# A fused Griffin block and two MLPs on one core: first part reordered, root on ScalarE, first x in four transfers

## The chip, the cores and the metric

The kernel runs on one core of a Trainium2 chip. The metric is the device time of one execution in microseconds (us). A core has these engines, each working through its own instructions in order: TensorE (PE, matrix products; PEld is its weight load), VectorE (DVE), ScalarE (ACT), GpSimd (POOL) and SyncE (SP), which here only issues transfers. They wait for each other through semaphores.

## What is computed

The reference, cut to its steps, for x of 4 sequences x 1024 tokens x 256 features:

```python
t = rmsnorm(x, norm1_w)
xb = causal_depthwise_conv(t @ Wx, conv_w, conv_b)          # 4 taps
r, i = sigmoid(xb @ Wa), sigmoid(xb @ Wi)
a = exp(-8 * softplus(lam) * r)
h = scan(a, sqrt(max(1 - a*a, 1e-12)) * (i * xb))           # h[s] = a[s] h[s-1] + b[s]
h1 = x + (h * gelu(t @ Wy)) @ Wo
u = rmsnorm(h1, norm2_w)
y = h1 + (gelu(u @ Wg) * (u @ Wu)) @ Wd                     # 256 -> 1024 -> 256
x1 = layernorm(x + y)
out = layernorm(x1 + relu(x1 @ W1 + b1) @ W2 + b2)          # 256 -> 1024 -> 256
```

## The kernel before

The tokens are cut into 8 chunks of 512 (four tiles of 128 tokens, two "pairs" of tiles). The hidden width of 1024 is cut into 8 units per chunk, so that gate, up and down of the first MLP are 64 units; a period is the 8 units of one chunk. Most products are done three times in a reduced type, as high x high, high x low and low x high part of the operands: `..._hi` is the rounded tensor (written by ACT, or by POOL for `gu_hi`), `..._lo` the rest (a subtraction on DVE). Six products of 512 columns (lines L361 to L363) are one `gate` or one `up` of a unit; 12 products of 256 columns (L372 to L374) are one `down`. The weights are split into hi and lo parts too, once, while the first chunk is worked on.

There is no scheduler: each engine's order is written by hand, one block per engine. It has a **front**, in which chunk 0 goes through the mixing part (norm, conv, gates a and i, scan, y, output projection) with plain fp32 products by halves of 256 tokens, and then the rounds. `first_period(r)`, r = 0 to 7, is period 0: units 0 to 7 of chunk 0, and between them the mixing of chunk 1 and the splits of the remaining weights. `round_of(r)` is each later round.

What stands in the front, engine by engine:

- SP: chunk 0's x in two transfers of 256 KB, one per pair, then six small vectors, Wx, then x of chunk 1 (`load_x(1)`, 512 KB, issue line L301) and the other weights.
- ACT: squares with row sums of the first x (L768), copy of the vectors, `lam` terms, then the first half of the transposed t scaled (`first_tT[0]`), then `square_second_x(0)`, which waits for x of chunk 1, and behind it in the queue `first_conv_start`, which begins the conv of chunk 0. Then tanh and exp for gate a and tanh for gate i by halves, the square root for the scan's input (L1093, with a table load before it), `first_tT[1]` half, gelu of y, and splits.
- POOL: mean and reciprocal root of the squares (`first_rms`, L1587 and L1590), `lam` constants, the norm of chunk 1, `first_rms` of h1, then `add_x_h1(0)` (x + h1 for the later sum, two adds of 128x512, L1639).
- DVE: the norm of t (L1148), the other half of `first_tT[0]`, 12 conv taps (L1199), scan input and scans (L1168, L1175), the product with y (L1183), h1 (`add_mix`, L1266), weight splits (`weight_lo`, L1353 and L1355), `uT_lo` (L1142).
- PE: `first_x`, `first_gates` (L447: for each half all of a, then all of i), transposes of chunk 1's t, y (L447 too), the x product of chunk 1 (`second_x`, L414), the output projection (`first_out`, L474), more of L414, the transposes of u (L388), then unit 0.

In `first_period(r)` PE does gate(r), up(r) and, from r = 1, down(r - 1). At r = 3 it then waits until Wa and Wi are split (`split_done("a", "i")`) and does `mix_decay(1)` and `mix_input(1)`, the gates of chunk 1. On DVE round r does `gate_times_up(r)` (L1308, waits for up(r) of PE and the gelu of ACT), `gate_lo(r)` (L1313, waits for POOL's `gu_hi`), and between them parts of chunk 1's conv; at r = 2 it splits Wa, Wi and Wx behind `gate_lo(2)`.

`LAG_UP` (10) and `LAG_DOWN` (11) say by how many rounds the second MLP's products follow.

Of the kernel before, what the change touches and what calls it, by code (L numbers as in the profile page):

```python
# [10 lines left out]
P = 128  # L11
# [14 lines left out]
def griffin_mlp_kernel(nc, x, norm1_w, Wx, Wy, conv_w, conv_b, Wi, Wa, lam, Wo, norm2_w, Wg, Wu, Wd,  # L26
# [14 lines left out]
    with ctx:  # L41
# [62 lines left out]
        ln_eps = sb("ln_eps", [P, 1])  # L104
        half_c = sb("half_c", [P, KD])
# [46 lines left out]
        def x_squares(c):  # L152
            return c + 2

# [53 lines left out]
        x0_loaded = [sem(f"x0_loaded{q}") for q in range(PAIRS)]  # L208
# [7 lines left out]
        second_tT_ready = sem("second_tT_ready")  # L216
# [35 lines left out]
        u_ready = sem("u_ready")  # L252
        xh_ready = sem("xh_ready")
# [28 lines left out]
        ln_eps_ready = sem("ln_eps_ready")  # L282
        last_sd_ready = sem("last_sd_ready")
# [15 lines left out]
        def _(sync):  # L299
# [5 lines left out]
            def load_first_x(q):  # L305
                sync.dma_start(xs[0][:, 2 * q:2 * q + 2, :],
                               x_dram[0:1, :, 2 * q:2 * q + 2, :].rearrange("c p t d -> (c p) t d")
                               ).then_inc(x0_loaded[q], DMA)
# [13 lines left out]
            for q in range(PAIRS):  # L322
                load_first_x(q)
# [34 lines left out]
        def _(pe):  # L358
# [24 lines left out]
            def transposed_by_pairs(src, c, ready, done, bank, fillers):  # L383
                for q in range(PAIRS):
                    pe.wait_ge(ready, 4 * c + 2 * q + 2)
# [37 lines left out]
            def first_x():  # L423
                for h in range(2):
                    for m in range(KD):
                        pe.wait_ge(first_tT_ready[h], KD)
# [4 lines left out]
                        for k in range(KD):  # L431
                            last = nc.tensor.matmul(psum[2 * m + h][:, 0:cols.stop - cols.start],
                                                    raw_weight("x")[:, k, m * P:(m + 1) * P],
                                                    first_tT[0][:, k, cols], start=(k == 0), stop=(k == KD - 1))
                        last.then_inc(half_wx_done if h == 0 else wx_done, 1)

            def second_x(m):
                pe.wait_ge(second_tT_ready, KD)
                pe.wait_ge(tanh_i_ready, KD)
                for k in range(KD):  # L440
                    last = raw_step(psum[MIX + m][:, :], "x", m, k, first_tT[1])
                last.then_inc(wx_done, 1)
# [9 lines left out]
            def first_gates(h):  # L452
                pe.wait_ge(w_loaded["a"], DMA)
                for k in range(KD):
                    pe.wait_ge(half_taps_added if h == 0 else taps_added, taps_done(0, LOOKBACK - 1, k))
                    last = half_step(SECOND, "a", k, h, xb)
                last.then_inc(wa_done, 1)
                pe.wait_ge(w_loaded["i"], DMA)
                for k in range(KD):
                    last = half_step(MIX, "i", k, h, xb)  # L460
                last.then_inc(wi_done, 1)
# [52 lines left out]
            def transpose_u(c):  # L514
                pe.wait_ge(u_ready, 4 * c + 4)
# [10 lines left out]
            def gate_up(r):  # L526
                c, m = divmod(r, KH)
# [8 lines left out]
                product(gate_bank(r)[:, :], "g", m, uT_hi, uT_lo).then_inc(gate_done, 1)  # L536
                if r == 0:
# [123 lines left out]
            def first_period(r):  # L661

                gate_up(r)
                if r in (1, 5):

                    pe.wait_ge(hi_split["d"], 1 + r // 5)
                    pe.wait_ge(lo_split["d"], 1 + r // 5)
                if 1 <= r < KH - 1:
                    down(r - 1)
# [4 lines left out]
                if r == KH - 1:  # L674
# [6 lines left out]
                    split_done("x")  # L681
                    mix_x(2, [0])
                    transposed_by_pairs(normed, 1, u_ready, uT_done, SECOND, (0, 0))
                    mix_x(2, [1])

            def round_of(r):
                p, m = divmod(r, KH)
                n = p + 1
                mixing = n < CHUNKS
                if units(r):  # L690
# [15 lines left out]
                if r in (LAG_DOWN, LAG_DOWN + 4):  # L706
# [1059 lines left out]
```

## Time and profile before

| what | us |
|---|---|
| median of 3 runs | 599.85 |
| lowest and highest run | 599.59, 600.19 |
| the profiled execution, its own time | 600.54 |
| its span, first to last instruction | 598.7 |
| PE busy in the span | 590.6 (99%) |
| DVE, ACT, POOL busy | 381.5, 317.2, 187.1 |

Times in the rows are microseconds from the span's start. A row of the timeline is one instruction or some equal ones that follow each other: start, time from the first one's start to the last one's end, engine, line, operation, out<-in with shapes, and in brackets how long the engine was idle before it and what ended that. Matmuls overlap, so a row of PE that lasts 0.39 can be followed by the next after 0.23; a wait of PE is seen best in the distance of two starts.

### The profile page before, as it was taken

The numbers are of one execution on the slowest core, as the hardware profiler recorded it, in microseconds if no ns is written. First come the engines' busy times: TensorE is split into PE (matmuls) and PEld (weight loads), VectorE is DVE, ScalarE is ACT, GpSimd is POOL, SyncE is SP. The second block draws the span as 40 slices with busy tenths as digits, with TensorE's granted clock in tenths as the row PEclk, the third lists the DMA queues.
The fourth block names the chain that finished last, engine by engine and source line by source line (L and its number), as shares of the span: only waits on it lengthen the run. The fifth ranks groups of instructions, "written<-read, shape, count | busy, mean of one in ns | idle before, by whom it ended". The sixth has DMA issues, their size and how long they took to land.

```text
span 598.7 us, 9284 instructions
## 1 busy us (share of the span) xinstructions
PE 590.6 (99%) x3529; PEld 521.7 (87%) x3529; DVE 381.5 (64%) x700; ACT 317.2 (53%) x601; POOL 187.1 (31%) x287
## 2 busy tenths in 40 slices
PE   8999999999999999999999999999999999999996
PEld 7768888899888998889898988889888898889896
DVE  5889877374856567484774846857478474662565
ACT  5988853654438444375443744356444653323454
POOL 3041353117240352313513153140722215240130
PEclk9999999999999999999999999999999999999999
DMA  8530010001001010010100001010000100010011
GB/s 283 166 106 1 1 36 1 2 1 36 1 1 35 2 37 0 1 36 2 35 2 19 18 1 36 1 36 2 1 1 0 37 2 0 2 36 0 1 37 36
DMA packets 13100, 15.68 MB, mean 26 GB/s; under 512 B 616, under 2 KB 12288, under 8 KB 13056
## 3 DMA queue, kind: packets, MB, share of 16 engines
q1 hardware_dynamic: 13056, 15.09, 7.5%
q8 instruction: 28, 0.46, 0.3%
q14 instruction: 16, 0.13, 0.1%
HBM read 10.89 MB, written 4.19 MB: 25 GB/s over the span
## 4 chain that ended last, share of the span: by engine, by line
PE 91%; DVE 5%; ACT 1%; issue 1%; DMA 1%; POOL 1%; SPq 0%; DVEq 0%
PE psum L361 17%; PE psum L363 17%; PE psum L362 17%; PE psum L372 11%; PE psum L374 11%; PE psum L373 11%; PE psum L379 3%; DMA xs<-in_L_attn_x_dram 1%; PE psum L447 1%; PE psum L575 1%; PE psum L577 1%; PE psum L573 1%; DVE row L1285 1%; PE psum L474 1%; PE psum L414 1%
## 5 line engine op out<-in xcount | busy, mean ns | idle before, releaser
L1662 POOL TENSOR_SCALAR gu_hi<-gu_raw 128x512 fp32r<-128x512 f32 x64 | 52.8, 824 | 313.1 <-DVE gu_raw L1308 310.3
L1318 DVE TENSOR_TENSOR hid_lo<-hid_raw,hid_hi 128x512 fp32r<-128x512 f32 x56 | 45.6, 814 | 84.0 <-ACT hid_hi L952 84.0
L948 ACT ACTIVATE hid_raw<-psum,vecs 128x512 f32<-128x512 f32 x56 | 38.5, 687 | 113.8 <-PE psum L363 113.8
L1308 DVE TENSOR_TENSOR gu_raw<-psum,gu_raw 128x512 f32<-128x512 f32 x64 | 44.1, 689 | 68.4 <-PE psum L363 68.1
L372 PE MATMUL psum<-w_d_hi,gu_hi 128*128 128x256 f32 x256 | 72.8, 284 | 0.2 <-DVE gu_lo L1313 0.2
L372 PE MATMUL psum<-w_hi,hid_hi 128*128 128x256 f32 x256 | 71.7, 280 | 0.2 <-DVE hid_lo L1318 0.2
L374 PE MATMUL psum<-w_hi,hid_lo 128*128 128x256 f32 x256 | 71.8, 281 | 0.0
L374 PE MATMUL psum<-w_d_hi,gu_lo 128*128 128x256 f32 x256 | 71.8, 281 | 0.0
L373 PE MATMUL psum<-w_lo,hid_hi 128*128 128x256 f32 x256 | 71.7, 280 | 0.0
L373 PE MATMUL psum<-w_d_lo,gu_hi 128*128 128x256 f32 x256 | 71.7, 280 | 0.0
L939 ACT ACTIVATE gu_raw<-psum 128x512 f32<-128x512 f32 x64 | 38.3, 598 | 48.6 <-PE psum L363 48.0
L1313 DVE TENSOR_TENSOR gu_lo<-gu_raw,gu_hi 128x512 fp32r<-128x512 f32 x64 | 44.5, 696 | 14.7 <-POOL gu_hi L1662 14.7
L361 PE MATMUL psum<-uT_hi,w_g_hi 128*128 128x512 f32 x128 | 51.1, 399 | 0.2 <-DVE uT_lo L1142 0.2
L372 PEld LDWEIGHTS psum<-w_hi,hid_hi 128*128 128x128 f32 x256 | 48.2, 188 | 3.2 <-DVE hid_lo L1318 0.6
L372 PEld LDWEIGHTS psum<-w_d_hi,gu_hi 128*128 128x128 f32 x256 | 48.2, 188 | 3.1 <-DVE gu_lo L1313 0.7
L361 PE MATMUL psum<-uT_hi,w_u_hi 128*128 128x512 f32 x128 | 50.0, 390 | 0.3 <-DVE w_u_lo L1353 0.2
L373 PEld LDWEIGHTS psum<-w_lo,hid_hi 128*128 128x128 f32 x256 | 48.1, 188 | 2.2
L363 PE MATMUL psum<-uT_hi,w_u_lo 128*128 128x512 f32 x128 | 50.0, 390 | 0.0
L362 PE MATMUL psum<-uT_lo,w_g_hi 128*128 128x512 f32 x128 | 50.0, 390 | 0.0
L363 PE MATMUL psum<-uT_hi,w_g_lo 128*128 128x512 f32 x128 | 49.9, 390 | 0.0
L362 PE MATMUL psum<-uT_lo,w_u_hi 128*128 128x512 f32 x128 | 49.8, 389 | 0.0
L373 PEld LDWEIGHTS psum<-w_d_lo,gu_hi 128*128 128x128 f32 x256 | 48.1, 188 | 1.9
(222 smaller groups left out, 1519.3 us busy)
## 6 DMA issues: line engine op xcount, KB each, us to landing
out_dram<-row SPq DMA_DIRECT2D x15, 256.0 KB, 2.2
xs<-in_L_attn_x_dram SPq DMA_DIRECT2D x7, 512.0 KB, 3.5
raw<-in_L_ffn_W_dram SPq DMA_DIRECT2D x2, 1024.0 KB, 7.9
raw_gud<-in_L_attn_Wg_dram SPq DMA_DIRECT2D x1, 1024.0 KB, 7.4
raw_gud<-in_L_attn_Wu_dram SPq DMA_DIRECT2D x1, 1024.0 KB, 9.5
raw_gud<-in_L_attn_Wd_dram SPq DMA_DIRECT2D x1, 1024.0 KB, 12.7
xs<-in_L_attn_x_dram SPq DMA_DIRECT2D x2, 256.0 KB, 2.9
raw_xyai<-in_L_attn_Wx_dram SPq DMA_DIRECT2D x1, 256.0 KB, 2.6
```

The lines of the kernel that those rows point to most:

```text
L361: nc.tensor.matmul(dst, w_hi[n][:, k, cols], hi[:, k, :], start=(k == 0), stop=False)
L362: nc.tensor.matmul(dst, w_hi[n][:, k, cols], lo[:, k, :], start=False, stop=False)
L363: return nc.tensor.matmul(dst, w_lo[n][:, k, cols], hi[:, k, :], start=False, stop=(k == KD - 1))
L372: nc.tensor.matmul(dst, hi, w_hi[n][:, k, :], start=start, stop=False, skip_group_check=True)
L373: nc.tensor.matmul(dst, hi, w_lo[n][:, k, :], start=False, stop=False, skip_group_check=True)
L374: return nc.tensor.matmul(dst, lo, w_hi[n][:, k, :], start=False, stop=stop, skip_group_check=True)
L939: nc.scalar.activation(gu_raw[:, r % SLOTS, :], gate_bank(r)[:, :], ACT.Gelu_apprx_tanh).then_inc(gelu_ready, 1)
L948: nc.scalar.activation(hid_raw[:, w % SLOTS, :], bank[:, :], ACT.Relu, bias=vec("b1", m)).then_inc(relu_ready, 1)
L1308: nc.vector.tensor_tensor(gu_raw[:, r % SLOTS, :], up_bank(r)[:, :], gu_raw[:, r % SLOTS, :], ALU.mult).then_inc(gu_ready, 1)
L1313: nc.vector.tensor_tensor(gu_lo[:, r % SLOTS, :], gu_raw[:, r % SLOTS, :], gu_hi[:, r % SLOTS, :].bitcast(FP32), ALU.subtract).then_inc(gu ...
L1318: nc.vector.tensor_tensor(hid_lo[:, w % SLOTS, :], hid_raw[:, w % SLOTS, :], hid_hi[:, w % SLOTS, :].bitcast(FP32), ALU.subtract).then_inc ...
L1662: nc.gpsimd.tensor_scalar(gu_hi[:, r % SLOTS, :], gu_raw[:, r % SLOTS, :], 1.0, 0.0, ALU.mult, ALU.add).then_inc(gu_hi_ready, 1)
```

## The change

The front:

- The first x comes in four transfers of 128 KB, tiles 0 and 2 from SP's queue, 1 and 3 from ACT's.
- The reciprocal root of the first x's mean square is a Sqrt on ACT and a reciprocal on DVE, instead of two POOL instructions. ACT gets a table load for Sqrt first and one for Exp behind the copy of the vectors.
- DVE and ACT exchange the halves of `first_tT[0]`; the `lam` steps of DVE come behind it.
- `first_gates` does a and i of feature half k together, k = 0 then k = 1. `second_x` is cut by k: k = 0 of both m before `first_out(0)`, k = 1 of m = 0 between the two `first_out`, k = 1 of m = 1 behind them.
- On DVE `first_scan_input(1)` and `first_scan(1, 0)` come later; the last tile of u's norm is done by DVE instead of ACT, ahead of `weight_lo("u", ks=[0])`.
- `add_x_h1(0)` of POOL moves from the end of the front behind `gate_hi(3)`.

Period 0 and after:

- PE does gate(1) before up(0), and down(r - 2) between gate(r) and up(r) instead of down(r - 1) behind up(r). The transposes of u of chunk 1 go by pairs around `mix_x(2, [0])`.
- Unit 11 has the order gate, down, up, then a, W1, i, W2; at unit 10 DVE takes `gate_times_up` earlier; `uT_lo` of chunk 1 stands before both statistics.

```diff
@@ SP: first x @@
-            for q in range(PAIRS):
-                load_first_x(q)
+            for tt in (0, 2):
+                load_first_x(tt)
@@ PE: first_gates @@
                 pe.wait_ge(w_loaded["a"], DMA)
+                pe.wait_ge(w_loaded["i"], DMA)
                 for k in range(KD):
                     pe.wait_ge(half_taps_added if h == 0 else taps_added, taps_done(0, LOOKBACK - 1, k))
-                    last = half_step(SECOND, "a", k, h, xb)
-                last.then_inc(wa_done, 1)
-                pe.wait_ge(w_loaded["i"], DMA)
-                for k in range(KD):
-                    last = half_step(MIX, "i", k, h, xb)
-                last.then_inc(wi_done, 1)
+                    last_a = half_step(SECOND, "a", k, h, xb)
+                    last_i = half_step(MIX, "i", k, h, xb)
+                last_a.then_inc(wa_done, 1)
+                last_i.then_inc(wi_done, 1)
@@ PE: first_period @@
-                gate_up(r)
-                if r in (1, 5):
-
-                    pe.wait_ge(hi_split["d"], 1 + r // 5)
-                    pe.wait_ge(lo_split["d"], 1 + r // 5)
-                if 1 <= r < KH - 1:
-                    down(r - 1)
+                if r != 1:
+                    gate(r)
+                if r == 0:
+                    gate(1)
+                if r in (2, 6):
+
+                    pe.wait_ge(hi_split["d"], 1 + r // 6)
+                    pe.wait_ge(lo_split["d"], 1 + r // 6)
+                if r >= 2:
+                    down(r - 2)
+                up(r)
@@ PE: end of the front @@
-            second_x(0)
+            for m in range(KD):
+                second_x(m, 0)
             pe.wait_ge(w_loaded["o"], DMA)
             for q in range(PAIRS):
                 first_out(q)
-            second_x(1)
+                second_x(q, 1)
@@ ACT: square_first_x @@
+                    act.wait_ge(rms_eps_ready, 1)
+                    act.wait_ge(x_squared, q + 1)
+                    nc.scalar.activation(rstd1[:, tiles], ss1[:, tiles], ACT.Sqrt, bias=rms_eps[:, :],
+                                         scale=1.0 / D).then_inc(rms1_ms, 1)
@@ ACT: front @@
+            for tt in (1, 3):
+                act.dma_start(xs[0][:, tt:tt + 1, :],
...
+            act.preload_act_table(ACT.Sqrt)
             square_first_x()
...
+            act.preload_act_table(ACT.Exp)
@@ DVE: first_norm_t @@
+                nc.vector.reciprocal(rstd1[:, tiles], rstd1[:, tiles]).then_inc(rms1_rstd, 1)
@@ DVE: front, scans @@
-            for h in range(2):
-                first_scan_input(h)
+            first_gated_input(1)
+            first_scan_input(0)
             for m in range(KD):
                 first_scan(0, m)
-            first_scan(1, 0)
+            first_scan_input(1)
             first_gated(0)
-            first_scan(1, 1)
+            for m in range(KD):
+                first_scan(1, m)
@@ DVE: front, end @@
             dve.wait_ge(rms2_rstd, 2)
+            dve.wait_ge(tT_done, 4)
+            nc.vector.tensor_scalar(normed[:, TT - 1, :], h1[0][:, TT - 1, :], rstd2[:, TT - 1:TT], None,
+                                    ALU.mult).then_inc(last_u_ready, 1)
             weight_lo("u", "n2", ks=[0])
@@ POOL: round_of @@
                     gate_hi(r)
+                    if r == 3:
+                        add_x_h1(0)
@@ POOL: front @@
             first_rms(0, ss2, h1_squared, rms2_ms, rstd2, rms2_rstd)
-            add_x_h1(0)
```

What stands in a row on PE where unit 0 ends and unit 1 begins; `psum0` and `psum4` take gate(0) and gate(1), `psum1` and `psum5` up(0) and up(1). Before:

```order
L363 MATMUL psum0<-uT_hi,w_g_lo 128x512
L361 MATMUL psum1<-uT_hi,w_u_hi 128x512
L362 MATMUL psum1<-uT_lo,w_u_hi 128x512
L363 MATMUL psum1<-uT_hi,w_u_lo 128x512
L361 MATMUL psum1<-uT_hi,w_u_hi 128x512
L362 MATMUL psum1<-uT_lo,w_u_hi 128x512
L363 MATMUL psum1<-uT_hi,w_u_lo 128x512
L361 MATMUL psum4<-uT_hi,w_g_hi 128x512
```

and after:

```order
L371 MATMUL psum0<-uT_hi,w_g_lo 128x512
L369 MATMUL psum4<-uT_hi,w_g_hi 128x512
L370 MATMUL psum4<-uT_lo,w_g_hi 128x512
L371 MATMUL psum4<-uT_hi,w_g_lo 128x512
L369 MATMUL psum4<-uT_hi,w_g_hi 128x512
L370 MATMUL psum4<-uT_lo,w_g_hi 128x512
L371 MATMUL psum4<-uT_hi,w_g_lo 128x512
L369 MATMUL psum1<-uT_hi,w_u_hi 128x512
```

gate(1) has moved in front of up(0).

PE in round 3, ahead of the gates of chunk 1 (`mT_hi`, `w_a_hi`); `psum3` takes down, `psum5` up(3). Before:

```order
L374 MATMUL psum3<-w_d_hi,gu_lo 128x256
L372 MATMUL psum3<-w_d_hi,gu_hi 128x256
L373 MATMUL psum3<-w_d_lo,gu_hi 128x256
L374 MATMUL psum3<-w_d_hi,gu_lo 128x256
L361 MATMUL psum6<-mT_hi,w_a_hi 128x512
```

and after:

```order
L371 MATMUL psum5<-uT_hi,w_u_lo 128x512
L369 MATMUL psum5<-uT_hi,w_u_hi 128x512
L370 MATMUL psum5<-uT_lo,w_u_hi 128x512
L371 MATMUL psum5<-uT_hi,w_u_lo 128x512
L369 MATMUL psum6<-mT_hi,w_a_hi 128x512
```

Ahead of `mix_decay(1)` stood three downs, the last right before it; now two stand there, and down(2) comes in round 4.

POOL at the end of the front and in period 0, `h_0` being the sum of x and h1 of chunk 0. Before:

```order
L1590 TENSOR_TENSOR rstd<-rstd,minus_half 128x2
L1639 TENSOR_TENSOR h_0<-h_0,xs 128x512 x2
L1625 COPY xtail<-xv 128x6
L1662 TENSOR_SCALAR gu_hi<-gu_raw 128x512 x6
L1595 TENSOR_SCALAR rstd<-ss 128x4
```

and after:

```order
L1657 TENSOR_TENSOR rstd<-rstd,minus_half 128x2
L1692 COPY xtail<-xv 128x6
L1731 TENSOR_SCALAR gu_hi<-gu_raw 128x512 x4
L1708 TENSOR_TENSOR h_0<-h_0,xs 128x512 x2
L1731 TENSOR_SCALAR gu_hi<-gu_raw 128x512 x2
```

The two adds have moved behind four of the `gu_hi`.

## Rows read from the trace of the kernel before

**Rows 1.** The page: its head and part 1, busy time of each engine.

```profile
span 598.7 us, 9284 instructions
PE 590.6 (99%) x3529; PEld 521.7 (87%) x3529; DVE 381.5 (64%) x700; ACT 317.2 (53%) x601; POOL 187.1 (31%) x287
```

**Rows 2.** Stretches from:to: length, busy us (instructions) by engine, PE clock, DMA share, GB/s.

```profile
38.00:82.00 44.00, 43.80 (x257) 38.29 (x258) 37.58 (x60) 34.91 (x68) 13.25 (x16) 1.00 0.09 35
82.00:110.00 28.00, 27.48 (x142) 22.59 (x142) 17.69 (x31) 12.81 (x23) 11.04 (x16) 1.00 0.06 19
110.00:560.00 450.00, 449.88 (x2716) 401.35 (x2715) 275.15 (x494) 220.65 (x407) 143.28 (x212) 1.00 0.04 13
```

**Rows 3.** The chain that ended last, in the front: start, us, engine, what.

```profile
4.09 4.87 DMA xs<-in_L_attn_x_dram
...
20.44 1.28 ACT L1093
21.73 0.64 ACT xv L1093
```

**Rows 4.** Timeline of the first 14 us, all engines.

```profile
3.52 0.42 ACT L768 ACTIVATE decay<-xs 128x256 f32<-128x256 f32 x1 [1.52 <-DMA xs<-in_L_attn_x_dram]
...
7.38 0.84 ACT L1076 ACTIVATE first_tT<-psum,vecs 128x256 f32<-128x256 f32 x2 [1.11 <-PE psum L388]
...
8.99 0.42 ACT L788 ACTIVATE inp<-xs 128x256 f32<-128x256 f32 x1 [0.77 <-DMA xs<-in_L_attn_x_dram]
...
12.14 1.10 PE L447 MATMUL psum<-xb,raw_xyai 128*128 128x256 f32 x4
...
13.47 0.70 PE L447 MATMUL psum<-xb,raw_xyai 128*128 128x256 f32 x2 [0.23 <-DVE xb L1199]
```

**Rows 5.** Timeline of 14 to 40 us, DVE at the end of the front.

```profile
25.65 0.67 DVE L1183 TENSOR_TENSOR gy<-gy,xv 128x512 f32<-128x512 f32 x1
...
30.26 0.69 DVE L1266 TENSOR_TENSOR h<-psum,xs 128x512 f32<-128x512 f32 x1
```

**Rows 6.** Timeline of PE from 36 us: units 0 and 1, and the first down.

```profile
36.08 0.54 PE L361 MATMUL psum<-uT_hi,w_g_hi 128*128 128x512 f32 x1
36.46 0.40 PE L362 MATMUL psum<-uT_lo,w_g_hi 128*128 128x512 f32 x1
...
37.38 0.39 PE L363 MATMUL psum<-uT_hi,w_g_lo 128*128 128x512 f32 x1
37.94 0.47 PE L361 MATMUL psum<-uT_hi,w_u_hi 128*128 128x512 f32 x1 [0.17 <-DVE w_u_lo L1353]
...
39.16 0.39 PE L363 MATMUL psum<-uT_hi,w_u_lo 128*128 128x512 f32 x1
...
41.88 0.39 PE L363 MATMUL psum<-uT_hi,w_u_lo 128*128 128x512 f32 x1
42.48 0.36 PE L372 MATMUL psum<-w_d_hi,gu_hi 128*128 128x256 f32 x1 [0.20 <-DVE gu_lo L1313]
```

**Rows 7.** Timeline of PE, 46 to 60 us: gate(3), down(2) and mix_decay(1) begin.

```profile
48.16 0.40 PE L361 MATMUL psum<-uT_hi,w_g_hi 128*128 128x512 f32 x1
...
50.89 0.28 PE L372 MATMUL psum<-w_d_hi,gu_hi 128*128 128x256 f32 x1
...
52.30 0.40 PE L361 MATMUL psum<-mT_hi,w_a_hi 128*128 128x512 f32 x1
```

**Rows 8.** Timeline of DVE, 38 to 60 us.

```profile
39.66 0.69 DVE L1308 TENSOR_TENSOR gu_raw<-psum,gu_raw 128x512 f32<-128x512 f32 x1
...
47.02 0.69 DVE L1308 TENSOR_TENSOR gu_raw<-psum,gu_raw 128x512 f32<-128x512 f32 x1 [0.35 <-PE psum L363]
...
50.64 0.69 DVE L1355 TENSOR_TENSOR w_i_lo<-raw_xyai,w_i_hi 128x512 fp32r<-128x512 f32 x1
...
54.39 2.35 DVE L1355 TENSOR_TENSOR w_lo<-raw,w_hi 128x1024 fp32r<-128x1024 f32 x2
```

**Rows 9.** Timeline of 141 to 147 us: the same adds of a later chunk beside DVE.

```profile
143.67 2.54 POOL L1639 TENSOR_TENSOR h<-h,xs 128x512 f32<-128x512 f32 x2
144.91 1.84 DVE L1318 TENSOR_TENSOR hid_lo<-hid_raw,hid_hi 128x512 fp32r<-128x512 f32 x1 [2.02 <-ACT hid_hi L952]
```

More of the change, by code:

```diff
@@ L381, in transposed, with transposed_by_pairs @@
                     last.then_inc(done, 1)
-            def transposed_by_pairs(src, c, ready, done, bank, fillers):
-                for q in range(PAIRS):
-                    pe.wait_ge(ready, 4 * c + 2 * q + 2)
+            def transposed_by_pairs(src, c, ready, done, bank, fillers, qs=range(PAIRS)):
+                for q in qs:
+                    if ready is u_ready:
+                        if c == 0 and q == 1:
+                            pe.wait_ge(last_u_ready, 1)
+                            pe.wait_ge(ready, u_tiles(0))
+                        else:
+                            pe.wait_ge(ready, u_tiles(c - 1) + 2 * q + 2)
+                    else:
+                        pe.wait_ge(ready, 4 * c + 2 * q + 2)
                     for tt in (2 * q, 2 * q + 1):
@@ L689, in round_of @@
                 mixing = n < CHUNKS
+                if r == LAG_DOWN:
+                    gate(r)
+                    down(r - 1)
+                    up(r)
+                    mix_decay(n)
+                    mlp_up(r - LAG_UP)
+                    mix_input(n)
+                    pe.wait_ge(hi_split["2"], 1)
+                    pe.wait_ge(lo_split["2"], 1)
+                    mlp_down(r - LAG_DOWN)
+                    return
                 if units(r):
@@ L1094, in _ @@
                                      scale=-0.25).then_inc(gate_ready, 1)
-            act.wait_ge(tT_done, 4)
-            nc.scalar.activation(first_tT[1][:, 1, :], psum[GATE + 1][:, :], ACT.Copy,
-                                 scale=vec("n1", 1)).then_inc(second_tT_ready, 1)
             act.preload_act_table(ACT.Gelu_apprx_tanh)
@@ L1101, in _ @@
                 nc.scalar.activation(gy[:, :, half(h)], pair_bank(DOWN, h), ACT.Gelu_apprx_tanh).then_inc(gy_ready, 1)
+                if h == 0:
+                    act.wait_ge(tT_done, 4)
+                    nc.scalar.activation(first_tT[1][:, 1, :], psum[GATE + 1][:, :], ACT.Copy,
+                                         scale=vec("n1", 1)).then_inc(second_tT_ready[1], 1)
             weight_hi("g", "n2", ks=[1])
@@ L1489, in lam_stepped @@
                 dve.wait_ge(lam_step, steps)
-            first_norm_t(0)
+            for q in range(PAIRS):
+                first_norm_t(q)
+            dve.wait_ge(vecs_ready, 1)
+            dve.wait_ge(tT_done, 1)
+            for f in range(KD):
+                nc.vector.tensor_scalar(first_tT[0][:, f, half(0)], pair_bank(MIX, 0)[:, f, :], vec("n1", f), None,
+                                        ALU.mult).then_inc(first_tT_ready[0], 1)
             dve.wait_ge(lam_exp, 1)
@@ L1499, in _ @@
             lam_stepped(nc.vector.scalar_tensor_tensor(poly, poly, series[3], z, ALU.add, ALU.mult))
-            dve.wait_ge(vecs_ready, 1)
-            dve.wait_ge(tT_done, 2)
-            for f in range(KD):
-                nc.vector.tensor_scalar(first_tT[0][:, f, half(1)], pair_bank(MIX, 1)[:, f, :], vec("n1", f), None,
-                                        ALU.mult).then_inc(first_tT_ready[1], 1)
             for c in (2, 1):
```

92 lines of the change are left out of this document (57 added, 35 removed).

## The prediction, made before the changed kernel was run

> **What bounds the kernel now.** I read the page first: PE is busy 590.6 of 598.7 us [rows 1]. The stretches then say where the rest is. From 110 to 560 us PE is busy 449.88 of 450 us, and the change touches nothing there [rows 2]; whatever the change gives or takes comes from the front (0 to 36 us, where unit 0 begins) and from period 0 and the start of period 1 (to some 110 us). In those the page of stretches shows 0.20 us of idle PE between 38 and 82, and 0.52 between 82 and 110 [rows 2]. Starts of products show more, since a product that waits is seen as lasting: after the one at 37.38 the next comes at 37.94 where it should come 0.23 later (0.33 lost), after 41.88 at 42.48 (0.37 lost), each with some 0.08 at the restart [rows 6]. So the removable waits at the start of period 0 are 0.41 + 0.45 = 0.86 us. The chain shows what sets the front: the transfer of chunk 1's x from 4.09 to 8.96 [rows 3], then ACT's squares at 8.99 and everything behind them; ACT had been idle 0.77 us there and the transfer ended it [rows 4].
>
> All terms are made against the profiled execution (600.54 us, span 598.7, so 1.84 around it) and then laid on the median 599.85.
>
> **The front up to the first x's use: nothing.** Taking the root off POOL brings the first norm forward by a part of a microsecond, and the four transfers may add to that. But ACT's next step that matters, the squares of chunk 1's x and the conv start behind them, cannot begin before 8.97 [rows 3, 4]. The transfers' order on SP is the same, so x of chunk 1 is issued and lands as before; it could land earlier or later by the traffic that now goes through ACT's queue, and the path would move with it one for one. I take 0, with -0.3 to +0.3. The added work on ACT is hidden under the same wait: one table load of 1.28 [rows 3] more, a Sqrt of a few elements twice, and two issues before the first load, while ACT waits for x anyway until 3.52 [rows 4]. Laid in a row from 3.52, four squares at 0.42 and two roots at some 0.25 with the second landing between them end near 5.9, the copy of the vectors at 6.05, the load at 7.35, the lam terms at 7.75, and the two copies of `first_tT` (0.84) at 8.6 [rows 4]: 0.37 us before 8.97. That margin is the cover; if the load took longer than 1.65, the excess would be on the path.
>
> The Trainium skill (page "ScalarE: Activation LUTs", section "What ACT_TABLE_LOAD costs") gives about 1.28 us for the load and another 1.38 us of drain for every switch of set. Here the load at 20.44 is followed by the activation at 21.73, 0.01 us after its end [rows 3], so the trace shows no drain; by the page's figure the load would end at 8.7, the copies at 10.0, and the front would be 1.0 us late instead of 0.
>
> **The rest of the front: near nothing.** Interleaving a and i removes PE's wait between the product groups at 12.14 and 13.47 (four products of two passes take 0.86, the fifth comes after 1.33: 0.47 lost) [rows 4]. But it puts two more groups of i (0.86 us) ahead of the end of a in the second half, so that a(1), on which tanh, exp, table load and Sqrt hang, comes 0.86 - 0.47 = 0.4 later. On DVE one scan of 0.67 us no longer stands before the product with y at 25.65, so this comes 0.67 - 0.4 = 0.3 earlier and the first output projection with it; the second one has 0.86 us of `second_x` before it, so it ends at about 30.5 and h1 of the second pair starts at 30.7 instead of 30.26 [rows 5]. The last norm tile on DVE beside ACT's gives these 0.4 us back. Then `uT_lo` of both pairs has to be done, behind a 1.28 us weight split that now starts later. I get the first product of unit 0 between 35.9 and 36.45 against 36.08, and take 36.08: **0 us**, with -0.3 and +0.4 as ends for the whole front.
>
> **Period 0: the place that decides.** Price of the steps: gate(3) begins at 48.16, down(2) at 50.89, so a gate or an up takes 2.73/2 = 1.365; down(2) to `mix_decay` at 52.30 is 1.41 [rows 7]. With gate(1) ahead of up(0), the last product of up(0) starts at 36.08 + 0.15 (restart, 36.08 to 36.46 instead of 0.23) + 17 x 0.2275 = 40.10 instead of 39.16 [rows 6]: 0.94 later. DVE's `gate_times_up(0)`, which waits for it, moves from 39.66 to 40.60 [rows 8]. Everything of DVE that follows is in one queue with little air: from 39.66 to the end of `w_i_lo` at 50.64 + 0.69 = 51.33 there are 11.67 us with one wait for PE, 0.35 at 47.02 [rows 8]. (Two waits of 0.5 for POOL's `gu_hi` are part of the chain and move with it.) So `w_i_lo` is done at 51.33 + 0.94 - 0.35 = 51.92.
>
> PE meanwhile: down(0) waits as before, since `gu_lo(0)` moves by the same 0.94 (42.48 to 43.42, PE there at 36.23 + 5 x 1.365 = 43.06; 0.36 and 0.08). PE then reaches `split_done("a", "i")` at 36.23 + 8 x 1.365 + 2 x 1.41 + 0.44 = 50.4, since down(2) no longer stands in front of it. It waits there until 52.0, **1.6 us**. Before, PE arrived at 52.30 [rows 7], 0.97 after `w_i_lo`, and did not wait. The balance: `mix_decay(1)` starts at 52.0 instead of 52.3, but 1.41 us of down(2) is still to be done, and the restart costs 0.08: 52.0 + 1.41 + 0.08 - 52.3 = **+1.2 us**. The wait for `w_u_lo` at 37.94 that the change removes (0.41) is inside this balance.
>
> **The moved adds.** POOL's two adds now start right after `gu_hi(3)`, about 53.4, beside DVE's `gu_lo(3)` and, from 54.39 on, the 128x1024 splits [rows 8], which is where DVE is late already. A subtraction of 128x512 beside the second of such adds lasted 1.84 instead of 0.69 [rows 8, 9]: 1.15 us for each add, at most 2.3 on DVE. In 38 to 82 us DVE is busy 37.58 of 44 [rows 2], and the downs, a unit later, need `gu_lo` later; so PE should see only a part. Ends 0 and 1.15; I take **+0.5**, under the middle since most of DVE's air lies after 60 us.
>
> The Trainium skill (page "SBUF — State Buffer", section "SBUF: two separate sides") says that VectorE with two inputs in SBUF and GpSimd exclude each other for a whole instruction. The 1.84 us row agrees [rows 9]; by that rule both adds are paid in full on DVE, 2.3 us, if each gets in between two splits.
>
> x of chunk 2 waits for these adds: SP issues it some 20 us later, near 57 instead of 36.8. Its square on ACT comes near 66, so 3.5 to 6 us of transfer stay hidden.
>
> **From unit 7 to unit 11.** The reorderings there move small waits about: 0.52 us of PE idle between 82 and 110 [rows 2] with restarts some 1.2. I take 0, with -0.5 and +0.5: down(10) ahead of up(11) waits for its `gu_lo` sooner, `uT_lo` before the statistics saves at most 0.4.
>
> **Sum:** 0 + 1.2 + 0.5 + 0 = +1.7 us, so 599.85 + 1.7 = **601.55**, and a profiled span near 600.4. Its ends: 0.4 to 3.2 above.
>
> **Rivals.**
> 1. Forecast, DVE's queue decides (0.50): 600.6 to 602.6.
> 2. The front gives something (0.15): a part of the first x in another queue lets x of chunk 1 land up to 1 us earlier, at 8.0. For it: ACT idled 0.77 for that transfer [rows 4]. Against: issue time and bytes are the same. Then 601.55 - 1.0 = 600.55.
> 3. Other side, faster (0.06): the wait at Wa and Wi doesn't come. Place: `split_done("a", "i")`; point: `w_i_lo` done before 50.4, which needs DVE's 11.32 us of work there to take 9.8. Then the waits at 37.94 and 42.48 (0.86) and those of 82 to 110 (0.5) are won: 599.85 - 1.4 = 598.5. Against: the durations are those of rows 8, and nothing in the change shortens them.
> 4. The adds are paid in full (0.14): 0.6 more, with down(10) 0.5 more, 602.7.
> 5. The second table load comes with a drain and ACT is late at 8.97 (0.05): 1.0 more, 602.5.
> 6. The parts cancel (0.10): front -0.4, adds 0, unit 7 to 11 -0.5, so 600.1.
>
> A difference under 0.2% (1.2 us) is about what a measurement of this kernel cannot tell from none. Slower by more than that, over 601.05: most of the forecast (0.42 of 0.50), cases 4 and 5, together 0.61, and a little of 2: 0.64. Within: 0.30. Faster: 0.06. The range that leaves out 2 in 10 is 600.2 to 602.8.
>
> **What would show it.** In the new profile: PE's first `mix_decay` product stands near 52.0 with an idle time before it ended by DVE `w_i_lo` (or the line of the splits); up(0) starts right behind gate(1), without a wait; `gate_times_up(0)` near 40.6; the chain goes through DVE from 40 to 52. POOL's adds near 54 stretch DVE's `gu_lo(3)` or `w_lo` rows to 1.8 and more. ACT still waits for x of chunk 1 near 8.9, and unit 0 starts within 35.8 to 36.5. I am wrong if unit 0 starts much before 35.8, if PE goes from up(3) into `mix_decay` without a gap, or if PE loses over 1 us at some other place, for instance at the output projection of chunk 1, where DVE's lag would appear last.

## The result, and the profile after

| kernel | median us | lowest to highest | executions | profiled execution | its span |
|---|---|---|---|---|---|
| before | 599.76 | 599.59 to 600.19 | 6 | 600.54 | 598.7 |
| after | 602.25 | 601.99 to 602.92 | 6 | 602.32 | 600.5 |

The changed kernel is slower: ratio 1.0041, 95% interval 1.0030 to 1.0051, 2.5 us. The forecast was 601.55, with 600.2 to 602.8.

The page after, its head and part 1:

```profile
span 600.5 us, 9292 instructions
PE 589.8 (98%) x3529; PEld 520.9 (87%) x3529; DVE 383.9 (64%) x703; ACT 317.4 (53%) x603; POOL 184.1 (31%) x284
```

PE does what it did [rows 1]; the span is 1.8 longer. The stretches, as in [rows 2] (length, then busy us and instructions of PE, PEld, DVE, ACT, POOL, clock, DMA share, GB/s):

```profile
38.00:82.00 44.00, 41.58 (x244) 36.06 (x243) 36.70 (x54) 33.34 (x66) 14.77 (x17) 1.00 0.08 31
82.00:110.00 28.00, 27.36 (x141) 22.21 (x140) 19.84 (x36) 11.71 (x22) 11.53 (x16) 1.00 0.06 19
110.00:560.00 450.00, 449.88 (x2717) 401.45 (x2716) 274.42 (x493) 221.77 (x408) 142.78 (x212) 1.00 0.04 13
```

Nearly all that PE loses lies between 38 and 82 us: 43.80 busy has become 41.58. Between 82 and 110 it is 0.12, and behind 110 nothing moved. Who it waited for (what waits, for what, us in total, times, longest):

```profile
PE psum L369 <- DVE w_i_lo L1417: 1.4, 1, 1.4
PE psum L380 <- DVE gu_lo L1375: 0.8, 3, 0.4
PE psum L369 <- DVE gu_raw L1370: 0.7, 1, 0.7
```

The two large ones in PE's timeline: in front of `mix_decay(1)`, as foretold in [rows 7], and one that was not in the sum, in front of up(7), some 21 us later:

```profile
49.63 0.39 PE L371 MATMUL psum<-uT_hi,w_u_lo 128*128 128x512 f32 x1
51.47 0.47 PE L369 MATMUL psum<-mT_hi,w_a_hi 128*128 128x512 f32 x1 [1.45 <-DVE w_i_lo L1417]
...
72.09 0.28 PE L382 MATMUL psum<-w_d_hi,gu_lo 128*128 128x256 f32 x1
73.10 0.49 PE L369 MATMUL psum<-uT_hi,w_u_hi 128*128 128x512 f32 x1 [0.73 <-DVE gu_raw L1370]
```

By starts the first costs 51.47 - 49.63 - 0.23 = 1.61 us, the second 73.10 - 72.09 - 0.12 = 0.89 and 0.11 at the restart. DVE, as in [rows 8]:

```profile
39.99 0.69 DVE L1370 TENSOR_TENSOR gu_raw<-psum,gu_raw 128x512 f32<-128x512 f32 x1 [1.55 <-PE psum L371]
...
50.53 0.68 DVE L1417 TENSOR_TENSOR w_i_lo<-raw_xyai,w_i_hi 128x512 fp32r<-128x512 f32 x1
...
53.68 1.78 DVE L1375 TENSOR_TENSOR gu_lo<-gu_raw,gu_hi 128x512 fp32r<-128x512 f32 x1
55.38 3.44 DVE L1417 TENSOR_TENSOR w_lo<-raw,w_hi 128x1024 fp32r<-128x1024 f32 x2
...
63.49 0.68 DVE L1370 TENSOR_TENSOR gu_raw<-psum,gu_raw 128x512 f32<-128x512 f32 x1
...
72.36 0.69 DVE L1370 TENSOR_TENSOR gu_raw<-psum,gu_raw 128x512 f32<-128x512 f32 x1
```

and POOL's adds beside it:

```profile
53.45 3.15 POOL L1708 TENSOR_TENSOR h<-h,xs 128x512 f32<-128x512 f32 x2
```

DVE idles 1.55 us at 39.99, because up(0) now comes after gate(1); then `gu_lo(3)` lasts 1.78 instead of 0.68 and the pair of splits 3.44 instead of 2.35 [rows 8]: 2.2 us for two adds.

**A measure used below.** Unit 0's first product stands at 36.08 in the profile of before and at 35.50 in that of after; that looks like a gain of 0.58 in the front. A new profile of the unchanged kernel (below) has it at 35.49. So I split each profiled time into unit 0's start and the rest. The rest comes from one profiled execution of each kernel. It repeats within some 0.1 us where the code behind the front is the same and nothing of the front reaches over unit 0 (before, before again and b2; after and f4; b1 and b3):

| kernel | median us | ratio to before (95%) | profiled us | unit 0 at | rest |
|---|---|---|---|---|---|
| before | 599.76 | | 600.54 | 36.08 | 564.46 |
| before again | 599.97 | 1.0001 (0.9992 to 1.0010) | 599.84 | 35.49 | 564.35 |
| after | 602.25 | 1.0041 (1.0030 to 1.0051) | 602.32 | 35.50 | 566.82 |
| e1 adds back | 601.24 | 1.0023 (1.0013 to 1.0032) | 601.81 | 36.11 | 565.70 |
| e2 down(2) early | 602.31 | 1.0040 (1.0026 to 1.0053) | 602.98 | 36.20 | 566.78 |
| e3 both | 600.11 | 1.0003 (0.9994 to 1.0011) | 599.94 | 35.32 | 564.62 |
| f1 front only | 600.48 | 1.0013 (1.0004 to 1.0021) | 600.32 | 35.62 | 564.70 |
| f2 order undone | 601.53 | 1.0031 (1.0019 to 1.0043) | 601.57 | 35.73 | 565.84 |
| f3 no swap | 600.00 | 1.0002 (0.9994 to 1.0011) | 600.00 | 35.72 | 564.28 |
| f4 x in two | 603.09 | 1.0054 (1.0041 to 1.0067) | 603.10 | 36.27 | 566.83 |
| b1 downs later | 599.39 | 0.9994 (0.9986 to 1.0003) | 599.58 | 35.61 | 563.97 |
| b2 x in four | 599.55 | 0.9995 (0.9986 to 1.0004) | 599.57 | 35.21 | 564.36 |
| b3 later and four | 599.10 | 0.9987 (0.9978 to 0.9996) | 599.12 | 35.17 | 563.95 |
| b4 swap alone | 600.78 | 1.0016 (1.0007 to 1.0025) | 600.78 | 35.51 | 565.27 |

The e and f kernels are the changed kernel with parts undone, the b kernels the kernel before with parts added. By the rest the change costs 566.82 - 564.4 = 2.4 us, all behind unit 0's start. If the rest is the same in the timed executions, 602.25 - 566.82 puts that start at 35.4 in those of after, and 599.76 - 564.4 at 35.4 in those of before.

### The profile page after: what moved, and what is told of

Read it like the earlier page. It is cut to its first block, busy times and chain, and to the rows that moved or that the text cites. A ratio compares the mean times of both kernels' runs of the same rounds, so it can differ in the third digit from the quotient of the medians.

```text
span 600.5 us, 9292 instructions
## 1 busy us (share of the span) xinstructions
PE 589.8 (98%) x3529; PEld 520.9 (87%) x3529; DVE 383.9 (64%) x703; ACT 317.4 (53%) x603; POOL 184.1 (31%) x284
## 4 chain that ended last, share of the span: by engine, by line
PE 88%; DVE 5%; issue 2%; ACT 2%; POOL 1%; DMA 0%; POOLq 0%; DVEq 0%; ACTq 0%
PE psum L369 17%; PE psum L371 16%; PE psum L370 16%; PE psum L380 11%; PE psum L382 10%; PE psum L381 10%; PE psum L387 3%; PE psum L465 1%; POOL gu_hi L1731 1%; PE psum L599 1%; PE psum L601 1%; PE psum L597 1%; DVE row L1347 1%; PE psum L491 1%; DVE gu_raw L1370 1%
```

## The experiments

The theory after these two profiles: from 40 to 72 us there is one queue, DVE's, and both new waits of PE are the same lateness seen twice. The rival is the way the prediction added up: every wait of PE is a loss of its own.

**The kernel before, once more.** No edit.

> The kernel before, unchanged. In the two profiled executions unit 0 starts 0.58 us earlier in the changed kernel (35.50 against 36.08), and x of chunk 1 lands 1.2 us earlier (7.76 against 8.97), while the profiled execution of before (600.54) stood 0.8 us above the median of its timed runs (599.76). Theory A: the front of before is as a rule faster than in that one profile; then this new profile shows x of chunk 1 landing before 8.5 and unit 0 starting near 35.5, with a span near 598.0, and the real gain of the new front is near 0. Theory B: the profile was typical and the front gains 0.6; then unit 0 starts again within 0.1 of 36.08. Timed: 599.8, ratio 1.000 within 0.0005 in both.

Unit 0 at 35.49, span 598.0: theory A. ACT's first square of chunk 1's x, which [rows 4] had at 8.99:

```profile
8.28 0.42 ACT L788 ACTIVATE inp<-xs 128x256 f32<-128x256 f32 x1 [0.40 <-DMA xs<-in_L_attn_x_dram]
```

The same transfer, issued at 4.07 instead of 4.09, landed at 8.26 instead of 8.97. From this square to unit 0 it is 27.1 to 27.2 us here, in before and in every profile of the new front; so this square is the clock of the front. In before and here it moves by the landing of one transfer. In the new front it waited for the transfer in f1, f3 and f4 only; in the other five profiles x had landed and ACT was still at its own copies (the part on the front below).

**e1, the adds back.**

```diff
@@ POOL @@
                     gate_hi(r)
-                    if r == 3:
-                        add_x_h1(0)
...
             first_rms(0, ss2, h1_squared, rms2_ms, rstd2, rms2_rstd)
+            add_x_h1(0)
             tail(1)
```

> The changed kernel with POOL's two adds of x and h1 of chunk 0 back where they stood, at the end of the front. Theory 1 (DVE's queue carries the loss from 40 to 73 us): the subtraction gu_lo(3) and the two 128x1024 splits, 1.78 and 3.44 us in the changed kernel, go back to 0.68 and 2.35, DVE is 2.2 us earlier at 63, and PE's wait of 0.9 (72.09 to 73.10) with its restart goes; the wait of 1.6 at the splits of Wa and Wi stays, since it lies ahead of the adds. 1.0 to 1.2 us faster than the changed kernel: 601.1 (600.9 to 601.4). Theory 2 (the stretched instructions fall into DVE's air, as the prediction half assumed, and the wait at 72 has another cause): DVE's rows shorten, PE's waits stay, under 0.4 us faster, 601.9 or more. Theory 3: the adds cost as much where they stood, by stretching the split of Wu to 1.85 as before: unit 0 not later, but up(0) waits; no gain.

DVE in the same places, and what the adds do where they now stand:

```profile
35.98 2.35 DVE L1415 SCALAR_TENSOR_TENSOR w_u_lo<-raw_gud,vecs,w_u_hi 128x1024 fp32r<-128x1024 f32 x1
...
54.31 0.68 DVE L1375 TENSOR_TENSOR gu_lo<-gu_raw,gu_hi 128x512 fp32r<-128x512 f32 x1
54.91 2.35 DVE L1417 TENSOR_TENSOR w_lo<-raw,w_hi 128x1024 fp32r<-128x1024 f32 x2
```

and PE's waits:

```profile
PE psum L369 <- DVE w_i_lo L1417: 1.5, 1, 1.5
PE psum L380 <- DVE gu_lo L1375: 0.8, 3, 0.4
```

1.0 us faster by the medians, 1.12 by the rest; the wait at 72 is gone and that for Wi is there: theory 1 by its numbers. Its first half, that DVE's queue carries the loss, holds for what the adds cost, but not for what e1 still loses (see e3). The adds still stretch one DVE instruction, by 1.1 us (`w_u_lo`, 1.27 in after), but DVE waits for up(0) just behind it and loses nothing.

**e2, down(2) early.** PE alone, adds as in after:

```diff
-                if r >= 2:
+                if r >= 2 and r != 4:
                     down(r - 2)
                 up(r)
                 if r == 3:
+                    down(2)
                     split_done("a", "i")
```

> The changed kernel with one down moved on PE alone: down(2) stands ahead of mix_decay(1) again, in the wait for Wi, and not in round 4. Theory 1 (DVE's queue is the bound through to 73 us): the wait of 1.6 before mix_decay goes (PE reaches it near 51.3, w_i_lo is done at 51.2), but PE then runs 1.4 earlier into a DVE that is where it was, and the wait at 72 to 73 grows from 1.0 to about 2.4: the time stays at 602.2 (602.0 to 602.5). Theory 2 (the waits add, each is a loss of its own, as the sum of the prediction had it): 1.4 to 1.5 us faster, 600.8.

This takes away the largest wait of the profile. 0.06 us slower by the medians, 0.04 faster by the rest: nothing. `mix_decay(1)` starts at 52.16, with a wait of only 0.25, and then:

```profile
66.44 0.36 PE L380 MATMUL psum<-w_d_hi,gu_hi 128*128 128x256 f32 x1 [0.35 <-DVE gu_lo L1376]
71.20 0.39 PE L380 MATMUL psum<-w_d_hi,gu_hi 128*128 128x256 f32 x1 [0.34 <-DVE gu_lo L1376]
73.78 0.50 PE L369 MATMUL psum<-uT_hi,w_u_hi 128*128 128x512 f32 x1 [0.89 <-DVE gu_raw L1371]
```

The 1.4 us that PE has won it waits out at three places. The first product of up(7) stands 73.78 - 36.20 = 37.58 behind unit 0, in after 73.10 - 35.50 = 37.60. The rival, that every wait counts for itself, is out for this kernel.

**e3, both edits.**

> The changed kernel with both edits: the adds back at the end of the front, and down(2) ahead of mix_decay(1). Theory 1 (one queue of DVE behind both waits): with the adds gone DVE is 2.2 earlier and PE, which otherwise would gain nothing from down(2), can use it: 2.0 to 2.4 us faster than the changed kernel, 600.0 (599.8 to 600.4), though the second edit alone gives 0. Theory 2 (independent losses): the sum of the two single runs, whatever they are.

PE's waits from 36 to 110:

```profile
PE psum L380 <- DVE gu_lo L1376: 0.8, 3, 0.4
```

The rest falls by 2.20, where e1 alone gave 1.12 and e2 alone 0.04: the two are not independent. The early down is worth 1.1 us once DVE is in time (e1 to e3, 1.08), and nothing while it is late. Read the other way, the adds cost 2.16 where down(2) stands early (e2 against e3), which is all that DVE loses by them, and 1.12 where it stands late.

So there are two limits side by side, and the later one counts. DVE's `gate_times_up(7)` in before, e1 and after:

```profile
74.28 0.68 DVE L1308 TENSOR_TENSOR gu_raw<-psum,gu_raw 128x512 f32<-128x512 f32 x1
```

```profile
74.62 0.68 DVE L1370 TENSOR_TENSOR gu_raw<-psum,gu_raw 128x512 f32<-128x512 f32 x1
```

```profile
76.03 0.68 DVE L1370 TENSOR_TENSOR gu_raw<-psum,gu_raw 128x512 f32<-128x512 f32 x1
```

Behind unit 0 that is 38.20, 38.51 and 40.53. In after DVE is 2.33 late and the rest 2.4 longer: DVE is the limit. In e1 it is only 0.31 late, since it has made up the remainder of its late start in its own idle time, but the rest is 1.3 longer: there PE is the limit, which idled before `mix_decay(1)` and still has down(2) to do. In every other changed kernel of the table, DVE's lateness at this place and the difference of the rest agree within 0.15 us.

**f1, the new front only.** The order of periods 0 and 1 and the place of the adds as in before.

> The new front alone: root on ScalarE, four transfers, a and i by steps, second_x by steps; the order of periods 0 and 1 and the place of POOL's adds are those of before. Theory 1 (the front gives nothing: the profiles so far differ by which of two speeds TensorE's transposes near 6 us have, 0.6 us apart, in both fronts): between 599.8 and 600.3. The split of w_u_lo beside the two adds lasts 2.35 here (1.85 in before), so up(0) waits some 0.6 instead of 0.33: up to 0.3 us slower than before. Theory 2 (the first two profiles told the truth, the front gains 0.6 and it was the rest that lost 3.1): 599.3 to 599.5.

The rest is 0.3 above before, and the wait foreseen is there:

```profile
37.97 0.47 PE L369 MATMUL psum<-uT_hi,w_u_hi 128*128 128x512 f32 x1 [0.72 <-DVE w_u_lo L1395]
```

where [rows 6] had 0.17 at 37.94. Theory 2 (the front gains 0.6) is out. The median is 0.2 above my range. 600.48 - 564.70 puts unit 0 at 35.8 in the timed executions, 0.4 later than in those of before or after; this profile shows 35.62, and I can't say why these executions lay later.

**f2, PE's order of period 0 undone.** The adds stay where the change put them.

```diff
-                if r != 1:
-                    gate(r)
-                if r == 0:
-                    gate(1)
...
-                if r >= 2:
-                    down(r - 2)
-                up(r)
+                gate_up(r)
...
+                if 1 <= r < KH - 1:
+                    down(r - 1)
```

> The changed kernel with PE's order in period 0 as before (gate and up in pairs, each down behind the next unit, three downs ahead of mix_decay(1)); the adds stay where the change put them. Theory 1 (DVE's queue carries the loss): gate_times_up(0) can start 1.0 to 1.3 us earlier than at 39.99, everything of DVE up to 72 moves with it, and since the stretched instructions stay, PE's wait moves: gone before mix_decay, some 1.6 to 2.0 near 72. 1.0 to 1.3 us faster than the changed kernel: 601.1. Theory 2 (waits add): all waits of 36 to 52 us, 2.1, less the ones of before there, 0.9, gone: 1.3 faster and the wait at 72 stays 1.0: 601.0 too; they differ in the profile, by the size of the wait near 72 us (1.6 or more, against 1.0).

0.98 by the rest, 0.7 by the medians. The profile shows whose queue it is:

```profile
65.01 0.36 PE L380 MATMUL psum<-w_d_hi,gu_hi 128*128 128x256 f32 x1 [1.10 <-DVE gu_lo L1370]
69.77 0.38 PE L380 MATMUL psum<-w_d_hi,gu_hi 128*128 128x256 f32 x1 [0.37 <-DVE gu_lo L1370]
```

No wait is left in front of `mix_decay(1)`; 1.10 and 0.37 (2.0 us by starts, with the restarts) have come at 64 and 69, earlier than the 72 that I had named, since with the old order the downs ask for `gu_lo` a unit sooner. Against e1, where the adds are back and the new order stays, f1 gives the same difference: 565.70 - 564.70 = 1.00, with the later orders undone too. So the order costs 1.0, with the adds in either place, but not by the same way: here DVE's `gate_times_up(7)` comes 0.97 earlier behind unit 0 than in after, and the rest follows it; from e1 to f1 it is PE's wait that goes.

**f3, what the reasons so far would build.** Adds back, down(2) early, gate(1) no longer ahead of up(0), the end of period 0 and period 1 as before.

> The changed kernel with four edits, the best order that the reasons so far give: adds back at the end of the front, down(2) ahead of mix_decay(1), gate(1) not ahead of up(0) (down(0) and down(1) still a unit later than before), and the order of period 1 and of the end of period 0 as before. The wait at down(0) (0.44 in both kernels) goes, since PE comes 1.4 us later to it; the wait of up(0) for w_u_lo is 0.6 again; DVE runs 0.5 earlier than with both edits alone (600.1); the later pieces give 0.2. Expected 599.6 (599.3 to 600.0). If DVE was not the bound there, or the later waits only move, it stays at 600.1.

600.00, not 599.6. Behind the front it is 0.1 below before (564.28). The wait at down(0) is gone, but up(0) waits 0.87 us by starts for `w_u_lo`, which the adds stretch, instead of the 0.6 that I had taken. Against e3, which differs by gate(1) ahead of up(0) and by the later orders, the rest is 0.34 lower.

**f4, the first x in two transfers.** SP's two transfers of before, in the changed kernel.

> The changed kernel with the first x in two transfers on SP's queue, as before, all else as changed. Theory 1 (the transfers give nothing: ACT is busy with the table load and the two copies until 8.4, so that x of chunk 1, landing at 7.76 to 8.1, is not waited for): x of chunk 1 lands between 8.0 and 9.0, ACT waits for it by 0 to 0.5, time 602.2 to 602.7. Theory 2 (the four transfers gain): 0.7 to 1.2 us slower, 603.0 or more.

0.84 slower than after, with the same rest: theory 2. x of chunk 1 landed at 9.13, and ACT waits for it again:

```profile
9.15 0.42 ACT L838 ACTIVATE inp<-xs 128x256 f32<-128x256 f32 x1 [0.47 <-DMA xs<-in_L_attn_x_dram]
```

So the four transfers do gain in the changed front, and something else in it gives that back (the part on the front below says what).

**b1, the downs later, alone on the kernel before.** In the kernel before, the changed kernel's later downs, with down(2) early as in e2 and without the swap (cut: the waits for Wd move along, from rounds 1 and 5 to 2 and 6):

```diff
-                gate_up(r)
...
-                if 1 <= r < KH - 1:
-                    down(r - 1)
+                gate(r)
...
+                if r >= 2 and r != 4:
+                    down(r - 2)
+                up(r)
                 if r == 3:
+                    down(2)
                     split_done("a", "i")
```

> The kernel before with one part of the change alone, mended: down(0) and down(1) a unit later, down(2) where it was, ahead of mix_decay(1), the downs from down(3) on a unit later; gate(1) not moved, front and adds as before. Unit 0's start is taken off the time, since it moves by up to 0.7 us from run to run with the landing of x; that leaves 564.4 for before. Theory 1 (DVE's queue is full but not late here, and the wait of 0.44 at down(0) is PE's own, so lagging the down wins it): 563.95, about 599.35 in all. Theory 2 (with PE 0.4 earlier DVE becomes the bound further on and takes it back near 63 to 72): 564.3 to 564.4, 599.7.

563.97 was measured for 563.95 expected. PE's waits from 36 to 110:

```profile
PE psum L361 <- DVE gu_raw L1317: 0.3, 1, 0.3
PE psum L361 <- DVE uT_lo L1151: 0.2, 1, 0.2
PE psum L361 <- DVE w_u_lo L1362: 0.2, 1, 0.2
```

The one for `gu_lo` at down(0) [rows 6] is gone and nothing has come for it.

**b2, the first x in four, alone on the kernel before.**

> The kernel before with the first x in four transfers from two queues, nothing else. The squares of chunk 1's x on ACT start where the front's clock starts (27.1 us before unit 0 in every profile so far); they wait for x of chunk 1 until 8.28 to 8.99 with two transfers, and for ACT's own copies until 7.9 to 8.2. Theory 1 (x of chunk 1 lands up to 0.8 earlier with four): 0.2 to 0.6 faster, 599.2 to 599.6. Theory 2 (in the timed runs x was hardly waited for, or the four only move where it lands by chance): within 0.1 of before, 599.75.

The median is 0.2 below before, within the interval; x of chunk 1 landed at 7.84. Over all profiles it landed at 8.26, 8.38, 8.51, 8.97 and 9.13 with two transfers and at 7.76 to 8.59 with four (five and nine profiles, means 8.65 and 8.07). By the means the four gain some 0.6 us in landing, though the two ranges overlap; this timing alone can't show it. Of an earlier square not all reaches unit 0 in this front: 27.35 us lie between them in b2 and 27.23 in b3.

**b3, both on the kernel before.**

> The kernel before with both: downs a unit later (down(2) ahead of mix_decay) and the first x in four transfers. If both theories 1 hold: the gains add, since one lies ahead of unit 0 and the other behind: 599.0 (598.8 to 599.3). If not, 599.4 or more.

599.10, ratio 0.9987 (0.9978 to 0.9996): the only kernel here whose interval lies below 1; the medians differ by 0.65 us. It keeps two parts of the change (the downs with down(2) put back ahead of `mix_decay(1)`) and leaves out the swap, the moved adds, the new root and the new orders.

**b4, gate(1) ahead of up(0), alone on the kernel before.**

```diff
-                gate_up(r)
+                if r != 1:
+                    gate(r)
+                if r == 0:
+                    gate(1)
+                up(r)
```

> The kernel before with gate(1) ahead of up(0) alone, the downs and everything else as before. The wait for w_u_lo (0.41) goes, gate_times_up(0) on DVE starts 0.94 later (40.6, with unit 0 at 36.08). Theory 1 (DVE's lateness is taken up by its own 0.35 and 0.23 of idle and by 0.4 us that PE has in hand at 71): within 0.15 of before, rest 564.3 to 564.5. Theory 2 (what DVE loses there PE loses later, one for one): rest 564.7 to 565.0, 0.3 to 0.6 slower.

0.87 by the rest, more than theory 2 asks, and at a place that I had left out:

```profile
42.86 0.36 PE L372 MATMUL psum<-w_d_hi,gu_hi 128*128 128x256 f32 x1 [1.56 <-DVE gu_lo L1324]
```

down(0) comes right behind unit 1 here, and its `gu_lo` hangs on up(0). PE waits 1.72 by starts instead of 0.37; less the 0.41 at `w_u_lo` that the swap saves, that is 0.94, the lateness of `gate_times_up(0)`. Neither theory had the place, but what DVE loses by the swap PE does lose one for one.

## Why the prediction was right, and where its steps were not

**The end** was right: slower, 0.7 us beyond the point, inside the range. The measured parts behind the front are the adds, +1.1 (after against e1), the order, +1.0 (e1 against f1), and +0.3 for what is left in f1 (564.70 against 564.4), where `w_u_lo` comes later; together the 2.4 of the table. This is one way to divide it; in another order of the steps the adds come to 2.16 (e2 against e3). The forecast had 0.5, 1.2 and 0. That the time fell into the range is in part luck: the adds were put too low, and two terms were added up that run side by side. With the adds at the 2.2 that DVE loses, the same sum would have said 1.2 + 2.2 = 3.4 above, 603.2.

**Front: 0, measured 0 to 0.4.** For after it is 0: 35.4 in the timed executions of both kernels. The profile's 35.50 against 36.08 would have told a gain of 0.6 that isn't there; "unit 0 starts within 35.8 to 36.5" was wrong as a sign to look for, because the row it rested on, 8.96 [rows 3], is one draw of a transfer that lands between 8.3 and 9.1. And "it could land earlier or later ... I take 0" hid two parts: the four transfers gain (f4 against after, 0.84), and the rest of the new front gives about as much back. The profiles say where that happens. In the seven profiles of the new front with four transfers x landed at 8.12 in the mean, but the square began at 8.63, since ACT's copies, which stand behind the second table load, ended between 8.28 and 9.20. In the four profiles of the old front with two transfers x landed at 8.53 and the square began at 8.55, the copies having ended between 7.88 and 8.22. What is won in landing is lost in ACT's queue. No run has the new front without the table load, so this rests on the profiles alone. The step on ACT's work held:

```profile
6.04 1.28 ACT L1126 ACT_TABLE_LOAD   x1
7.34 0.20 ACT L1128 ACTIVATE sp<-vecs 128x2 f32<-128x2 f32 x1
7.68 0.82 ACT L1133 ACTIVATE first_tT<-psum,vecs 128x256 f32<-128x256 f32 x2
8.39 0.41 ACT L838 ACTIVATE inp<-xs 128x256 f32<-128x256 f32 x1
```

The copies end at 8.50, foretold 8.6; but x had landed at 7.76, so these copies are now what the square waits for. The load ends at 7.32 and the next activation starts at 7.34: no drain, rival 5 is out. (The Trainium skill's 1.38 us of drain, page "ScalarE: Activation LUTs", section "What ACT_TABLE_LOAD costs", shows in no row here.)

**The rest of the front: 0, right.** From ACT's square to unit 0: 27.09 before (27.21 in e0), 27.11 after. That is right for the sum; its single parts were not measured.

**Period 0: the rows right, the balance right only where it stands alone.** With unit 0 0.58 earlier, `gate_times_up(0)` was foretold at 40.02 and stood at 39.99; `w_i_lo`'s end at 51.34, and it was 51.21; the wait at `split_done("a", "i")` 1.6, and it was 1.61. (DVE waits for POOL's `gu_hi` three times in that stretch, not twice; they move with the chain, so the sum holds.) The balance, PE's wait of 1.6 less what this puts right elsewhere, gave 1.2. With the adds back it is what costs the time: from e1 to e3 only down(2) moves, and 1.08 us are won. With the adds where the change put them it is not: e2 takes the same wait away and gets 0.04. There the order costs by DVE, which starts its queue 0.9 later behind up(0) and has only some 0.6 us of idle time of its own up to 72; f2 makes it 0.97 earlier and gets 0.98. The sum of the prediction put a plus between this term and the next, where two limits stand side by side.

**The adds: 0.5, measured 1.1; the step that failed.** The duration was right (2.2 us on DVE, foretold at most 2.3). Wrong was "PE should see only a part ... since most of DVE's air lies after 60 us". The 6.4 us of DVE's idle time in [rows 2] was read as air; but from 42 to 63 us it waited for POOL's `gu_hi`, which is part of its own chain, once 0.35 for PE [rows 8], and once 0.23 for ACT, at 61.72. PE sees all of it when nothing else holds it up: 2.16 (e2 against e3). That it was 1.12 between e1 and after is not due to DVE's air, but to PE's own wait at `mix_decay(1)`, behind which the other 1.1 us are hidden. Rival 4, the adds in full at 1.15 us, is near what happened: it named 602.7. (By the rule of the Trainium skill, page "SBUF — State Buffer", section "SBUF: two separate sides", one of the two engines keeps the other out for a whole instruction; after and e1 agree, with 1.1 us for each DVE instruction that met an add, where an add takes 2.54 / 2 = 1.27.)

**Unit 7 to unit 11: 0.** No run has these orders alone. By the starts of PE's products 1.9 to 2.0 us are lost from 80 to 110 in after, e1, e2, e3 and f2, which have them, and 1.7 to 1.8 in before, f1 and f3, which have not; undoing them together with the period's order (e1 to f1, 1.00) gave no more than undoing that order alone (after to f2, 0.98). So I estimate 0 to 0.2, inside the -0.5 to +0.5.

**The other rivals.** The front's gain of 1.0 and the wait that doesn't come did not happen; the parts did not cancel.

## What to carry to other kernels

Before adding up waits of the bound engine, ask which of them end on the same queue. While that queue is late they are one lateness seen at several places: taking one away only moves it down the line (e2, 0). But relieving the queue uncovers the bound engine's own wait behind it (e1, which won 1.1 of the 2.2), and both edits together win all (e3, 2.2 for 1.1 + 0). Two limits side by side are not a sum: the later one counts, and each price has to be taken with the other limit named. Count as air only idle time in which the engine waits for something outside its own chain.

A stage that hangs on one transfer has a spread of its own. Take its start off each time before comparing what lies behind: here that cut a difference of 0.7 us between two profiles of the same kernel to 0.1.

An operation that feeds a full queue should not be put later to hide a smaller wait: gate(1) ahead of up(0) saved 0.41 at one place and cost 1.35 at another (b4, where down(0) comes right behind unit 1). Where the downs come a unit later, leaving it out won at most 0.34 (e3 against f3).

## What the runs showed of the hardware

One transfer of 512 KB, with the same transfers ahead of it and issued within 0.03 us, landed between 8.26 and 9.13 in five profiles.

POOL's two adds last 2.54 us in [rows 9], where one DVE instruction with two operands in SBUF ran beside them and was itself stretched to 1.84; in after, where two DVE instructions were stretched, they last 3.15, and in e1 3.28. Each of these DVE instructions took some 1.1 longer (`gu_lo` and the pair of splits in after, `w_u_lo` in e1). In e1 the subtraction that reads PSUM keeps its length while the adds run:

```profile
33.96 3.28 POOL L1708 TENSOR_TENSOR h<-h,xs 128x512 f32<-128x512 f32 x2 [0.69 <-ACT normed L983]
34.78 1.28 DVE L1200 TENSOR_TENSOR uT_lo<-psum,uT_hi 128x512 fp32r<-128x512 f32 x2
```

The 128x128 transposes of PE start 0.21 us apart at first and 0.11 apart from some point on, in all fourteen profiles. From 1.9 to 4.4 us they are 0.21 apart everywhere. The point lies near 4.6 us in e0 and near 7.6 in before, which are the same program, near 7.5 in e1 and e2, and in between in the others. Four transposes near 6 us took 0.60 in after (first row), 1.06 in e1 (second row), with the same code up to there:

```profile
5.91 0.60 PE L404 MATMUL psum<-ident,normed 128*128 128x128 f32 x4
```

```profile
6.04 1.06 PE L404 MATMUL psum<-ident,normed 128*128 128x128 f32 x4
```

The factor of two is that between TensorE's levels of 2.4 and 1.2 GHz. Yet the stretch from 6 to 7 us shows a granted clock of 1.00 in both, so that it is the clock is not shown. PE had been busy without a gap since 1.5 us in both. The slower ones put ACT's copies at 8.27 instead of 7.68 and unit 0 at 36.11 instead of 35.50, although x had landed at 8.10. Why the point lies earlier in one execution than in another stayed open.
